# Cross-attention in front of a routed feed-forward layer: packing the V product two heads to a strip and normalising it before the output projection

## What is computed

```python
x = x + _L0_xattn_ref(_layernorm(x), ctx, ctx, Wq, Wk, Wv, Wo)
# in _L0_xattn_ref
scores = einsum('bhse,bhte->bhst', qh, kh) / sqrt(D)
attn = softmax(scores, axis=-1)
out = einsum('bhst,bhtd->bshd', attn, vh).reshape(B, S, E)
return out @ Wo.T
```

## Time and profile before

| | |
|---|---|
| median of 3 runs | 2591.99 us |
| lowest and highest run | 2583.87 and 2592.43 us |
| profiled execution, first to last instruction | 2592.7 us (its whole time is not given) |
| mean granted clock of TensorE | 0.918 |

### The profile page before, as it was taken

The page is one execution under the profiler, slowest core; times in us unless marked ns, Lnnn a source line. Parts: engine busy times, 40 slices in busy tenths (PEclk is TensorE's granted clock), DMA queues, the critical chain, the costliest instruction groups (busy, mean ns, idle before and its releaser), DMA issues. The chain is left out here.

```text
span 2592.7 us, 55875 instructions
## 1 busy us (share of the span) xinstructions
PE 2097.7 (81%) x20646; PEld 1577.2 (61%) x20646; DVE 1587.4 (61%) x4387; ACT 1257.4 (48%) x2364; POOL 1216.0 (47%) x1648
## 2 busy tenths in 40 slices
PE   5888888988888888888888788999999889983310
PEld 3656565666656566666666567777777777762210
DVE  3566666666666666666665436666666666636556
ACT  3444445444544554444544336666666666650000
POOL 1034444443444444444444537777777777760000
PEclk8999999999999999999999699999999999996665
DMA  8244554545454545445453467777777777879999
GB/s 264 83 159 147 166 164 150 175 148 181 147 176 126 170 144 171 143 159 160 145 168 130 166 222 238 251 238 253 234 260 249 234 253 232 267 247 360 381 392 363
DMA packets 365486, 538.93 MB, mean 208 GB/s; under 512 B 100129, under 2 KB 297762, under 8 KB 361122
## 3 DMA queue, kind: packets, MB, share of 16 engines
q1 hardware_dynamic: 313186, 384.81, 46.6%
q0 software_dynamic: 52032, 150.54, 15.4%
HBM read 236.93 MB, written 298.32 MB: 206 GB/s over the span
## 5 line engine op out<-in xcount | busy, mean ns | idle before, releaser
L1076 POOL DMA_INDIRECT xs<-xn,idx x512 | 502.2, 981 | 605.4 <-DVE xn L922 149.5
L1101 POOL DMA_INDIRECT yt<-yo,ix x572 | 551.7, 965 | 188.9 <-issue 146.4
L686 ACT ACTIVATE pr<-A 128x512 f32<-128x512 f32 x512 | 264.4, 602 | 400.4 <-PE A L520 400.4
L817 DVE TENSOR_REDUCE ms<-A 128x4 f32<-128x512 f32 x512 | 316.8, 682 | 76.3 <-PE A L496 75.2
L600 PE MATMUL A<-ident,xr 128*128 128x128 f32 x1400 | 193.8, 283 | 79.0 <-DMA xr<-xs 61.4
L642 PE MATMUL A<-wt,hh 128*128 128x256 f32 x1144 | 249.4, 301 | 0.0
L600 PEld LDWEIGHTS A<-ident,xr 128*128 128x128 f32 x1400 | 163.3, 145 | 136.6 <-DMA xr<-xs 89.2
L642 PE MATMUL A<-wsh,act 128*128 128x256 f32 x512 | 130.4, 413 | 126.7 <-DVE rr L992 126.7
L956 DVE TENSOR_TENSOR xl<-A,xh 128x512 fp32r<-128x512 f32 x286 | 184.0, 683 | 76.0 <-ACT xh L737 75.0
L516 PE MATMUL A<-qt,km 32*128 32x128 f32 x4096 | 229.0, 343 | 0.6 <-DVE mt L837 0.6
L516 PEld LDWEIGHTS A<-qt,km 32*128 32x128 f32 x4096 | 190.6, 218 | 54.2 <-issue 49.1
(11 more groups left out here) (146 smaller groups left out, 4147.8 us busy)
## 6 DMA issues: line engine op xcount, KB each, us to landing
xr<-xs SPq DMA_DIRECT2D x143, 576.0 KB
xs<-empty SPq DMA_DIRECT2D x36, 2048.0 KB, 10.7
gb<-yt SPq DMA_DIRECT2D x32, 2048.0 KB, 15.4
xb<-in_x SPq DMA_DIRECT2D x32, 512.0 KB, 6.3
cg<-in_ctx_t SPq DMA_DIRECT2D x32, 512.0 KB, 4.0
yd<-xb SPq DMA_DIRECT2D x32, 512.0 KB, 3.5
x2d<-xn SPq DMA_DIRECT2D x32, 512.0 KB, 3.0
xr<-x2d SPq DMA_DIRECT2D x32, 512.0 KB
```

The source lines that it names most:

```text
L686: ac(pr[:, 4 * b:4 * b + 4, :].rearrange("p h s -> p (h s)"), banks[4 + b][:, :], ACT.Exp, scale=SCALE)\
L817: v.reduce_max(ms[n % 2][:, b, 0:4], banks[b][:, :].rearrange("p (h t) -> p h t", h=4), AX.X)\
L1076: q.indirect_dma_start(xs, bass.IndirectOffsetOnAxis(ap=idx[:, n, k:k + 1], axis=0), x2[g % 4][:, i, :], None).then_inc(sent[g % 4], 16)
L1101: q.indirect_dma_start(yt, bass.IndirectOffsetOnAxis(ap=ix[:, n % 8, k:k + 1], axis=0), yo[n % 4][:, k, :], None).then_inc(put[n % 4], 16)
```

## The change

The V projection of two neighbouring heads 2j and 2j+1 is laid out in `vp` so that each has 32 columns of which its own 16 are at different places: the even head in the first half, the odd one in the second, the rest zero. In PV the two matmuls of a pair add up in the same strip, which then holds 32 useful rows, and the product of all 16 heads fills 256 columns of bank 5 in the layout that the projection wants. The other 256 columns get the softmax sums: for each head another matmul of the same shape with a constant `half` as weights, ones in the 16 columns of the even or odd head, so that each sum stands in the 16 rows of its head. VectorE takes the reciprocal of these 128x256 values and multiplies straight from the bank into `ot`. OTR, OT and ScalarE's two copies go. MT moves from bank 5 to bank 7. The scatters' third and fourth wait are for MT and OP in place of OTR and OT. VectorE's LN1 gets a wait for its own earlier aggregation.

```diff
--- before.py
+++ after.py
@@ -38,8 +38,8 @@
 LATE = 8
 
 
-ATT_BANKS = {"S": [0, 1, 2, 3], "K0": [4], "K1": [6], "Q0": [4], "Q1": [6], "VA": [4], "VB": [6], "PV": [5], "OTR": [7],
-             "MT": [5], "OT": [7], "XT": [1, 2], "XT2": [1, 2], "RL": [1], "RK": [1], "OP": [0], "ST": [4, 5, 6, 7]}
+ATT_BANKS = {"S": [0, 1, 2, 3], "K0": [4], "K1": [6], "Q0": [4], "Q1": [6], "VA": [4], "VB": [6], "PV": [5],
+             "MT": [7], "XT": [1, 2], "XT2": [1, 2], "RL": [1], "RK": [1], "OP": [0], "ST": [4, 5, 6, 7]}
 FFN_BANKS = {"TR": lambda u: [0, 1], "U": lambda r: [2 + r % 2], "DN": lambda u: [4 + 2 * (u % 2), 5 + 2 * (u % 2)]}
 
 
@@ -58,16 +58,16 @@
         out += [("S", n + 1), ("SC", s), first, ("PV", n), ("SC", s + 1)]
         if i == 2:
             out.append(("NA1", g + 2))
-        out += [second, ("OTR", n)]
+        out.append(second)
         if i == 0:
             out.append(("NA2", g - 1))
-        out += [("SC", s + 2), third, ("OT", n), ("SC", s + 3), ("MT", n + 1), ("OP", n), ("ST", n + 1)]
+        out += [("SC", s + 2), third, ("SC", s + 3), ("MT", n + 1), ("OP", n), ("ST", n + 1)]
         out += after
     g = G
     out += [("RK", g - 2), ("R2", g - 2), ("NA2", g - 1), ("XT2", g - 1), ("RL", g - 1), ("R1", g - 1), ("RK", g - 1), ("R2", g - 1)]
     out += [("SC", k) for k in range(TOPK * (B - 2 * GT - 1), TOPK * B)]
     last = {"SC": TOPK * B, "S": B, "MT": B, "ST": B, "VA": 2 * G, "VB": 2 * G}
-    return [(name, n) for name, n in out if 0 <= n < last.get(name, B if name in ("PV", "OTR", "OT", "OP") else G)]
+    return [(name, n) for name, n in out if 0 <= n < last.get(name, B if name in ("PV", "OP") else G)]
 
 
 def ffn_units():
@@ -210,9 +210,8 @@
         mb = sa("mb", [P, NH], BF16)
         ms = [sa(f"ms{k}", [P, 4, 32]) for k in range(2)]
         mt = [sa(f"mt{k}", [P, P], BF16) for k in range(2)]
-        osb = sa("osb", [P, 4, P])
-        rd = sa("rd", [P, NH])
-        o = sa("o", [P, NH, HD])
+        half = sa("half", [P, 2, HW])
+        rd = sa("rd", [P, KC * P])
         ot = sa("ot", [P, KC, P])
         stage = [sa(f"stage{k}", [P, 1, 2, E]) for k in range(2)]
         st1, mv1, ve1, rs1 = sa("st1", [P, GT, 6]), sa("mv1", [P, GT, 2]), sa("ve1", [P, GT]), sa("rs1", [P, GT])
@@ -500,13 +499,13 @@
 
             def MT(n):
                 pe.wait_ge(m_lo, n + 1)
-                wait_free(pe, 5, "MT", n)
-                tr(banks[5][:, 0:P], ms[n % 2][:, :, :].rearrange("p b k -> p (b k)"), ident[:, :])\
-                    .then_inc(fill[5], 1)
+                wait_free(pe, 7, "MT", n)
+                tr(banks[7][:, 0:P], ms[n % 2][:, :, :].rearrange("p b k -> p (b k)"), ident[:, :])\
+                    .then_inc(fill[7], 1)
 
             def ST(n):
                 g, i = divmod(n, GT)
-                wait_drained(pe, 5, "MT", n)
+                wait_drained(pe, 7, "MT", n)
                 for b in range(4):
                     wait_free(pe, 4 + b, "ST", n)
                 for r in range(4):
@@ -526,30 +525,19 @@
                 stg = "VA" if i % 2 == 0 else "VB"
                 wait_drained(pe, 4 if i % 2 == 0 else 6, stg, 2 * g + i // 2)
                 wait_free(pe, 5, "PV", n)
-                for b in range(4):
-                    wait_drained(pe, 4 + b, "ST", n)
-                    for q in range(4):
-                        h = 4 * b + q
-                        ins = mm(banks[5][32 * q:32 * q + 32, b * P:(b + 1) * P], vp[g % 2][:, i, h, :], pr[:, h, :],
-                                 start=True, stop=True)
+                for c in range(KC):
+                    wait_drained(pe, 4 + 2 * c, "ST", n)
+                    wait_drained(pe, 5 + 2 * c, "ST", n)
+                    for off, w in ((0, None), (KC * P, half)):
+                        for e in range(2):
+                            for q in range(4):
+                                h = 8 * c + 2 * q + e
+                                ins = mm(banks[5][32 * q:32 * q + 32, off + c * P:off + (c + 1) * P],
+                                         vp[g % 2][:, i, h, :] if w is None else w[:, e, :], pr[:, h, :], start=e == 0, stop=e == 1)
                 ins.then_inc(fill[5], 1)
 
-            def OTR(n):
+            def OP(n):
                 wait_drained(pe, 5, "PV", n)
-                wait_free(pe, 7, "OTR", n)
-                for b in range(4):
-                    ins = tr(banks[7][:, b * P:(b + 1) * P], osb[:, b, :], ident[:, :])
-                ins.then_inc(fill[7], 1)
-
-            def OT(n):
-                wait_drained(pe, 7, "OTR", n)
-                flat = o[:, :, :].rearrange("p h d -> p (h d)")
-                for c in range(KC):
-                    ins = tr(banks[7][:, c * P:(c + 1) * P], flat[:, c * P:(c + 1) * P], ident[:, :])
-                ins.then_inc(fill[7], 1)
-
-            def OP(n):
-                wait_drained(pe, 7, "OT", n)
                 wait_free(pe, 0, "OP", n)
                 for c in range(KC):
                     ins = mm(banks[0][:, 0:E], ot[:, c, :], wos[:, c, :], start=c == 0, stop=c == KC - 1)
@@ -589,7 +577,7 @@
             pe.wait_ge(const_set, 1)
             pe.wait_ge(w_in, 96)
             run(ATT, {"K0": K0, "K1": K1, "Q0": Q0, "Q1": Q1, "VA": VA, "VB": VB, "XT": XT, "S": Sc, "MT": MT, "ST": ST,
-                      "PV": PV, "OTR": OTR, "OT": OT, "OP": OP, "XT2": XT2, "RL": RL, "RK": RK})
+                      "PV": PV, "OP": OP, "XT2": XT2, "RL": RL, "RK": RK})
 
             def TR(u):
                 pe.wait_ge(xr_in[u % 3], 16 * (u // 3 + 1))
@@ -686,14 +674,6 @@
                     ac(pr[:, 4 * b:4 * b + 4, :].rearrange("p h s -> p (h s)"), banks[4 + b][:, :], ACT.Exp, scale=SCALE)\
                         .then_inc(drain[4 + b], 1)
 
-            def PV(n):
-                wait_filled(act_e, 5, "PV", n)
-                ac(osb[:, :, :].rearrange("p b s -> p (b s)"), banks[5][:, :], ACT.Copy).then_inc(drain[5], 1)
-
-            def OT(n):
-                wait_filled(act_e, 7, "OT", n)
-                ac(ot[:, :, :].rearrange("p c s -> p (c s)"), banks[7][:, 0:E], ACT.Copy).then_inc(drain[7], 1)
-
             def R1(g):
                 wait_drained(act_e, 1, "RL", g)
                 wait(act_e, r1, 6 * g)
@@ -717,7 +697,7 @@
                         .then_inc(xn2_ready, 1)
 
             act_e.wait_ge(const_set, 1)
-            run(ATT, {"NA1": NA1, "NA2": NA2, "K0": K0, "K1": K1, "Q0": Q0, "Q1": Q1, "XT": XT, "XT2": XT2, "ST": ST, "PV": PV, "OT": OT, "R1": R1})
+            run(ATT, {"NA1": NA1, "NA2": NA2, "K0": K0, "K1": K1, "Q0": Q0, "Q1": Q1, "XT": XT, "XT2": XT2, "ST": ST, "R1": R1})
 
             def WC(t):
                 if t == 0:
@@ -776,20 +756,22 @@
             v.memset(one16[:, :], 1.0)
             for a in (base, bound, shift, taken):
                 v.memset(a[:, :], 0.0)
+            v.memset(half[:, :, :], 0.0)
             v.memset(mask[:, 0:1], 0.0)
             v.memset(mask[:, 1:2], 1.0).then_inc(const_dve, 1)
             dve.wait_ge(const_dve, 3)
             for q in range(4):
                 v.memset(mask[32 * q:32 * q + HD, 0:1], 1.0)
                 v.memset(mask[32 * q:32 * q + HD, 1:2], 0.0)
-            for k in range(2):
-                v.memset(vp[k][:, :, :, HD:HD + 1], 1.0)
+            for e in range(2):
+                v.memset(half[:, e, e * HD:(e + 1) * HD], 1.0)
             dve.wait_ge(const_pool, 3)
             v.tensor_copy(lowb[:, :], lower[:, :])
             v.tensor_copy(sel[:, :, :], sel32[:, :, :]).then_inc(const_set, 1)
 
             def LN1(g):
                 dve.wait_ge(x_in[g % 2], 16 * (g // 2 + 1))
+                wait(dve, ln1_mv, g)
                 for i in range(GT):
                     ins = v.bn_stats(st1[:, i, :], xb[g % 4][:, i, :])
                 ins.then_inc(ln1_st, 1)
@@ -799,10 +781,11 @@
                     ins = v.bn_aggr(mv1[:, i, :], st1[:, i, :])
                 ins.then_inc(ln1_mv, 1)
 
-            def values(n, half, b, stg):
+            def values(n, one, b, stg):
                 g, k = divmod(n, 2)
                 wait_filled(dve, b, stg, n)
-                v.tensor_copy(vp[g % 2][:, 2 * k + half, :, 0:HD], banks[b][:, 0:E].rearrange("p (h d) -> p h d", h=NH))\
+                own = vp[g % 2][:, 2 * k + one, :, :].rearrange("p (j e) (w d) -> p j (e w) d", e=2, d=HD)[:, :, 0:4:3, :]
+                v.tensor_copy(own, banks[b][:, 0:E].rearrange("p (j e d) -> p j e d", e=2, d=HD))\
                     .then_inc(drain[b], 1)
 
             def VA(n):
@@ -824,17 +807,16 @@
                 dve.wait_ge(m_hi, n + 1)
                 v.tensor_tensor(ms[n % 2][:, :, 4:8], m4, bf, ALU.subtract).then_inc(m_lo, 1)
 
-            def OTR(n):
-                wait_filled(dve, 7, "OTR", n)
-                src = banks[7][:, :].rearrange("p (h w) -> p h w", h=NH)
-                v.reciprocal(rd[:, :], src[:, :, HD]).then_inc(rd_ready, 1)
+            def PV(n):
+                wait_filled(dve, 5, "PV", n)
```

(13 more changed lines are left out.)

## The result

The changed kernel takes 2628.16 us in the median, against 2588.79 us for the kernel before: a ratio of 1.0156, interval 1.0118 to 1.0194. It is slower by about 39 us, or 1.6%. The forecast was 2609 us, slower by 0.7%, with a range to 2642. The profiled execution took 2646.1 us, its span is 2644.4 us: 18 us above the median, so its waits are on the high side.

What follows compares the result with a forecast made beforehand. TensorE, busy for 81% of the span, was taken as the busiest engine, with the load of x tipping a draw per batch. Later groups' 13 us plus first groups' 4 gave +17, so 2610; forecast 2609 us, range 2572 to 2642.

Steps and rivals of the forecast that it cites:

- rival B: VectorE's wide reciprocal takes 2.4 us, lengthening its chain and the loop of x: +28 us, 2637 us; chance 0.13.
- Added to TensorE: In the product with V, 16 more matmuls with constant weights: +1.01 us per batch, upper bound 2.0 us.
- VectorE: Reciprocal grows from 128x16 (253 ns) to 128x256, estimated 1.75 us; VectorE gets 1.5 us more per batch.
- C: Rival: short reciprocal of 0.42 us, but NA2 still 1.0 us late; about 2597 us; chance 0.12.
- First batch: First batch of a group: OP waits for VectorE's reciprocal and multiply, starting at 806.97 instead of 806.57, +0.40 us.
- second batch: Second batch of a group: +0.05 us on top of the inherited 0.40; in the first 16 groups the loss is given back.
- Fourth batch: Fourth batch of a group: OP about 6.7 us after its score matmuls start, 6.88 before; -0.2 us.
- The load of x: SyncE's queue: NA2 ends 1.0 us later, x lands 15 to 16.6 us after it; loop of x +0.75 us.
- Sum: Whole kernel: 15 later groups at 0.85 us, 13, and 17 first groups at 0.25 us, 4; together +17 us.
- about 0.5 us appears in half of them: First 16 groups, where VectorE has no wait for x now: a new wait of about 0.5 us in half.
- Scatter: GpSimd's third and fourth scatter of a batch wait for MT and OP, up to 2 us later, at no cost.
- Rival A: Load hides the change and TensorE's clock holds, with fewer lower-clock stretches: faster, about 2557 us; chance 0.17.

Runs made afterwards that it cites:

- e1: Changed kernel with the load of x issued one batch group earlier, ahead of SyncE's wait for NA2: 2559.09 us, ratio 0.9874.
- e2: Kernel before with the load of x issued one batch group earlier: 2565.29 us, ratio 0.9905.
- e3: Changed kernel with NA2 moved ahead on ScalarE to before the product with V, SyncE's queue unchanged: 2561.2 us, ratio 0.9894.
- e7: Changed kernel with x asked for one group earlier and the router's softmax (R1) one place earlier, before ST: 2438.51 us, ratio 0.9413.
- e8: Kernel before with x asked for one group earlier and the router's softmax (R1) one place earlier: 2541.29 us, ratio 0.9812.
- e6: Changed kernel with x asked for one group earlier and half of the sum matmuls left out: 2565.75 us, ratio 0.9898.
- e10: Changed kernel with x asked for one group earlier, R1 moved earlier and half of the sum matmuls left out: 2446.74 us, ratio 0.9446.

## Why the prediction was right, and where it was not

The sign and its cause were right: with x out of the way the change is a draw (e1 and e2 lie 6 us apart), and the load of x behind a later NA2 makes it slower (e1 and e3 take 69 and 67 us off). The size was not right: 17 us were forecast and 39 measured. The time lies above the forecast's own range of 2600 to 2625 us and inside the whole range only because that reached up to rival B's side, for a slow reciprocal which did not come; so that it lies in the range is luck. Point by point:

- *Added to TensorE*, 1.01 us more per batch: 0.88.
- *VectorE*, reciprocal 1.75 us from two small rows: 1.750. B and C are out by this row.
- *First batch*: a wait of about 1.9 us before OP and 0.7 before MT; 1.79 and 1.10. OP comes 7.72 us after the router's first instruction in the later groups, where it came at 7.08: +0.64 for a forecast of +0.40. In the first fifteen it is 8.79 against 7.96, and the second batch gives it back, as forecast (20.45 against 20.59).
- *Fourth batch*: OP at about 6.7 us after the scores; 6.63. It still waits 0.55 us there, and in some later groups 0.63 in the second batch, where the prediction had hardly any wait.
- *The load of x*: NA2 was to end 1.0 us later in the group; 0.9. x was to arrive 15 to 16.6 us after it; 16.3 in the group shown. VectorE's total wait rose from 13.5 to 29.0 us in this stretch. The mechanism held in most groups, in the first half too.
- *Sum*: +17 us, measured +39. The term that failed is "about 0.5 us appears in half of them", +0.25 us for each of the first 17 groups. (The sum counts the 0.5 us in all 17; in half of them, as it says, it would be nothing in place of 4 us.) The waits there were 0.9 to 2.0 us, in eleven of the first fifteen groups, and set TensorE idle once more before OP of the third batch. In eight of them the clock then fell for a second time in the group. The prediction priced a wait at its own length. With the fall behind it, such a group was 2.5 to 5.3 us longer than the 44.3 us of before, and without it 0.7. The mean of the first fifteen is +2.0 us. For the later groups 0.85 us were forecast, and 1.2 measured.
- The kernel before already had this price in a row beside one that the prediction used. Its group with the wait of 3.12 us for x runs from 799.49 to 847.00, 47.5 us, and that is 5.6 longer than the undisturbed 41.95. OP of its third batch takes 2.08 us:

```profile
830.08 2.08 PE L555 MATMUL A<-wos,ot 128*128 128x256 f32 x4 [0.26 <-ACT ot L695]
...
847.00 0.22 DVE L874 TENSOR_REDUCE rsum<-ex 128x4 f32<-128x64 f32 x1 [2.40 <-ACT ex L700]
```

- *Scatter* at nothing: no run tests it.
- *Rival A* is out: the lower clock grew instead of shrinking.

What the prediction missed on the other side is how much the removed waits are worth once VectorE is in time: it took them as 0.3 to 0.9 us a batch less 0.3 us of work, a draw, because VectorE was late in the first batch in both kernels. With that lateness mended and x ahead (e7, e8) the same change is worth 103 us, of which the collision with NA2 in e8 may be a part. Its own working already had the row for it: VectorE comes to the maxima of the first batch after 2.40 us of idle time, and the prediction used that row only to count groups.

## What to carry to other kernels

Moving work later on an engine's list also moves every transfer that waits for that engine: the change lengthened one matmul group by 0.9 us and paid at a load that shared no data with it. Price a wait together with what the clock does after it: two groups with nearly the same wait for x (1.58 and 1.46 us) were 2.8 us apart here, by one fall. And a change that only pays where another engine arrives in time can look like a loss; find that engine's own idle time first (here 2.4 us for an exponential queued behind four others).

## What was not expected of the hardware

An element of the reciprocal costs 6.2 ns in this kernel (178 ns for 4, 253 for 16, 1750 for 256 per partition), while the multiply of 256 takes 424 ns, so repeating each sum over 16 rows raised the reciprocal from 253 to 1750 ns.

Less work on TensorE did not make the kernel faster, twice (e6 and e10). In both pairs the kernel with less work waits longer before OP and has the lower mean clock over its span: 0.907 in e6 against 0.913 in e1, and 0.936 in e10 against 0.940 in e7.
